# Ordering a tile's twelve matmuls by precision part, and moving four low-rank terms from VectorE to ScalarE and an accumulating store

## The reference

```python
def reference(x, itok_B_3_7, itok_B_0_15, L0_cond_A, L0_cond_B, L1_cond_W, L1_cond_lora_A, L1_cond_lora_B):
    ...
    x = x + _L0_cond_ref(x, L0_cond_A, L0_cond_B, itok_B_3_7)
    x = x + _L1_cond_ref(x, itok_B_0_15, L1_cond_W, L1_cond_lora_A, L1_cond_lora_B)
    return x
```

## Time and profile before

| | us |
|---|---|
| median of 3 runs | 1306.52 |
| lowest, highest | 1306.44, 1308.64 |
| the profiled execution | 1306.84 |
| its span, first to last instruction | 1305.1 |
| TensorE busy | 1293.8 (99%) |
| VectorE busy | 957.0 (73%) |
| ScalarE busy | 459.3 (35%) |
| GpSimd busy | 161.5 (12%) |

### The profile page before, as it was taken

How to read it: one execution, slowest core, us unless ns; L and a number is a source line. 1 busy time by engine, 2 the same in 40 slices (tenths; PEclk the granted TensorE clock), 3 DMA queues, 4 the chain that set the end, 5 groups by cost and what they waited for, 6 DMA issues and landing times.

```text
span 1305.1 us, 15493 instructions
## 1 busy us (share of the span) xinstructions
PE 1293.8 (99%) x5716; PEld 1068.6 (82%) x5716; DVE 957.0 (73%) x1031; ACT 459.3 (35%) x540; POOL 161.5 (12%) x277
## 2 busy tenths in 40 slices
PE   9999999999999999999999999999999999999998
PEld 7888888888888888888888888887888888888776
DVE  4547766556684786877677866769898887778998
ACT  3322222222234422332232443334433344444451
POOL 3001120111033210001201100111000110100021
PEclk9999999999999999999999999999999999999999
DMA  8786877669999965668978473572965987868577
GB/s 282 273 295 198 312 255 223 230 220 320 358 350 236 288 225 194 210 225 298 360 239 314 160 258 121 190 253 99 262 220 197 369 261 212 229 168 264 122 202 201
DMA packets 87549, 316.33 MB, mean 242 GB/s; under 512 B 15650, under 2 KB 15650, under 8 KB 81074
## 3 DMA queue, kind: packets, MB, share of 16 engines
q1 hardware_dynamic: 61010, 246.44, 54.7%
q0 software_dynamic: 26464, 68.90, 19.1%
HBM read 213.48 MB, written 102.83 MB: 242 GB/s over the span
## 4 chain that ended last, share of the span: by engine, by line
PE 85%; DVE 8%; DMA 2%; issue 2%; ACT 1%; POOLq 0%; POOL 0%; DVEq 0%; ACTq 0%
PE ps L1340 42%; PE ps L2510 33%; PE ps L1289 3%; PE ps L1247 2%; PE ps L2466 2%; DVE xq L2241 1%; PE ps L1268 1%; DVE b_lo L2260 1%; DMA out_y<-stage 1%; DVE w_lo L2254 1%; PE ps L2452 1%; DMA out_y<-stage_all 1%; DVE uq L2285 1%; DVE xq L2228 1%; DVE stage L2288 0%
## 5 line engine op out<-in xcount | busy, mean ns | idle before, releaser
L1340 PE MATMUL ps<-b_hi,w_hi 128*128 128x512 f32 x888 | 345.8, 389 | 0.4 <-DVE w_lo L968 0.4
L1340 PE MATMUL ps<-b_hi,w_lo 128*128 128x512 f32 x888 | 345.5, 389 | 0.0
L1340 PE MATMUL ps<-b_lo,w_hi 128*128 128x512 f32 x888 | 345.4, 389 | 0.0
L2510 PE MATMUL ps<-b_hi,w_hi 128*128 128x512 f32 x784 | 305.7, 390 | 3.0 <-DVE w_lo L2254 1.5
L2510 PE MATMUL ps<-b_hi,w_lo 128*128 128x512 f32 x784 | 305.1, 389 | 0.0
L2510 PE MATMUL ps<-b_lo,w_hi 128*128 128x512 f32 x784 | 305.0, 389 | 0.0
L1340 PEld LDWEIGHTS ps<-b_hi,w_hi 128*128 128x128 f32 x888 | 166.7, 188 | 35.7 <-DVE w_lo L968 1.3
L1340 PEld LDWEIGHTS ps<-b_hi,w_lo 128*128 128x128 f32 x888 | 166.7, 188 | 34.9
L1340 PEld LDWEIGHTS ps<-b_lo,w_hi 128*128 128x128 f32 x888 | 166.7, 188 | 34.6
L2087 ACT CAST w_hi<-wq 128x1024 fp32r<-128x1024 f32 x98 | 103.4, 1055 | 210.3 <-PE ps L2510 197.4
L2510 PEld LDWEIGHTS ps<-b_hi,w_hi 128*128 128x128 f32 x784 | 147.1, 188 | 35.6 <-DVE w_lo L2254 2.3
(11 more groups left out here) (186 smaller groups left out, 1283.6 us busy)
## 6 DMA issues: line engine op xcount, KB each, us to landing
x_raw<-in_xT SPq DMA_DIRECT2D x56, 512.0 KB, 6.9
wq<-w_ops SPq DMA_DIRECT2D x28, 1024.0 KB, 5.0
w_raw<-in_W SPq DMA_DIRECT2D x55, 512.0 KB, 6.0
xq<-in_xT SPq DMA_DIRECT2D x44, 512.0 KB, 6.1
out_y<-stage POOLq DMA_DIRECT2D x38, 512.0 KB, 5.7
w_sum<-x_raw SPq DMA_DIRECT2D x24, 512.0 KB, 8.4
out_y<-stage_all POOLq DMA_DIRECT2D x48, 256.0 KB, 6.2
wq<-w_sum SPq DMA_DIRECT2D x12, 1024.0 KB, 7.4
```

Of the source, the lines that this page charges most:

```text
L1340: last = pe.matmul(bank[:, :], w[n % 2][:, c, t * P:(t + 1) * P], x[:, 2 * j + c, :], start=(j == 0 and c == 0 and w is w_hi and x is b_hi ...
L2510: last = pe.matmul(out, w[:, h, c, col:col + P], b[x], start=(po in (Q1, Q2, Q5, Q3) and c == 0 and i == 0), stop=(c == 3 and i == 2), ski ...
```

## The change

Two parts, both in `two_level`.

1. In the first tile of each unit (t even) TensorE runs its 12 matmuls as four of high x high, four of low weights x high input, four of high weights x low input. It waits for w_hi and b_hi of the whole unit at the start, for w_lo before the fifth and for b_lo before the ninth matmul. In the second tile the order stays as it was.
2. The four low-rank terms of batch 6, tiles 0 to 3 (they belong to C11 of the last outer product; units (M5, 3) and (M5, 4)) change from kind "u2" to kind "hbm". VectorE's four `lr_add` go, ScalarE copies the four tiles, and GpSimd adds them to y by two accumulating stores, which stand three units after the matmul, in (M5, 6) and (M5, 7), and wait until both of C11's stores of y have landed (`u_stored[c]` at 32). `fin` of C11 no longer waits for `lr_add`.

```diff
+    fix_plan += [(6, 2 * h, unit(M5, 3 + h)) for h in range(2)]
...
-    for c, place in ((C11, 6), (C22, 10), (C12, 18), (C21, 22)):
+    for c, place in ((C22, 10), (C12, 18), (C21, 22)):
...
             pool.wait_ge(lr_copied, 2 * f + 2)
-            pool.wait_ge(stage_stored[GROUP[M2][c]][h], 16 * stage_stores(M2, c, h))
+            if b > 5:
+                pool.wait_ge(u_stored[c], 32)
+            else:
+                pool.wait_ge(stage_stored[GROUP[M2][c]][h], 16 * stage_stores(M2, c, h))
...
-                    if use[2] == n - 1:
+                    if use[2] == n - (3 if use[0] > 5 else 1):
                         store_fix(f)
...
-            dve.wait_ge(*sides(M5, c, h, False))
+            if c != C11:
+                dve.wait_ge(*sides(M5, c, h, False))
...
-                pe.wait_ge(w_ready, F + n + 1)
...
-                    for c in range(4):
-                        if t == 0 and c % 2 == 0:
-                            pe.wait_ge(x_ready, X0 + 2 * q + c // 2 + 1)
-                        if c == 3:
+                    hi, x_lo, w_lo_ = (w_hi, b_hi), (w_hi, b_lo), (w_lo, b_hi)
+                    if t % 2:
+                        terms = [(c, *pair) for c in range(4) for pair in (hi, x_lo, w_lo_)]
+                    else:
+                        terms = [(c, *pair) for pair in (hi, w_lo_, x_lo) for c in range(4)]
+                        pe.wait_ge(w_hi_done, F + n + 1)
+                        pe.wait_ge(x_hi_done, X0 + 2 * q + 2)
+                    for i, (c, w, b) in enumerate(terms):
+                        if t % 2 == 0 and i == 4:
+                            pe.wait_ge(w_ready, F + n + 1)
+                        if t % 2 == 0 and i == 8:
+                            pe.wait_ge(x_ready, X0 + 2 * q + 2)
+                        if i == 9:
                             for s in lr_here(n, t % 2, "bank"):
                                 lr_mm(s, out)
```

More of the change, by code:

```diff
@@ L2500, in rest @@
                             pe.wait_ge(*pair)
-                    for c in range(4):
-                        if t == 0 and c % 2 == 0:
-                            pe.wait_ge(x_ready, X0 + 2 * q + c // 2 + 1)
-                        if c == 3:
+                    hi, x_lo, w_lo_ = (w_hi, b_hi), (w_hi, b_lo), (w_lo, b_hi)
[11 more added lines that the diff above has]
+                        if i == 9:
                             for s in lr_here(n, t % 2, "bank"):
                                 lr_mm(s, out)
-                        x = (slice(None), 2 * (q % 2) + c // 2, c % 2, slice(None))
                         col = t % 2 * P
[L2509 to L2512, removed]
+                        last = pe.matmul(out, w[:, h, c, col:col + P], b[:, 2 * (q % 2) + c // 2, c % 2, :],
+                                         start=(po in (Q1, Q2, Q5, Q3) and i == 0), stop=(i == 11),
+                                         skip_group_check=po in CHAIN or mo in (M4, M5))
                     last.then_inc(tile_done, 1)
```

## The result

The changed kernel takes **1313.22 us** (median of 8 runs, 1311.02 to 1315.26) against 1306.48 for the kernel before in the same comparison (8 runs, 1306.32 to 1309.11). The ratio is 1.0045, with a 95% interval of 1.0037 to 1.0054: slower by 5.9 us (the two medians alone differ by 6.7). The profiled execution took 1313.49 us, 1311.5 of them in the span.

What follows compares the result with a forecast made beforehand. TensorE, busy 1293.8 of 1305.1 us, bounds the kernel, with VectorE's queue setting the end from 1260 us. A late load's +4.2 less 0.97 gained gives +3.2 over 1306.52: 1309.7 us, range 1304.0 to 1312.8.

Steps and rivals of the forecast that it cites:

- High parts first: First tiles: w_lo gaps at (M7, 1) and (M5, 5) close, -0.97 and -1.02 us; waits already met cost 0.
- from this part alone: At (M5, 5): the new matmul order by itself closes the w_lo gap, -1.02 us.
- C11 to ScalarE, relief of VectorE: In M5: 2.4 us leave VectorE's queue, its lead shrinks to 1.1 us, and an earlier store of stage gives 0.3.
- The landing of C11's second store of y: On GpSimd's queue: it lands at 1261.9 instead of 1264.2, bounds 1260.0 and 1263.0.
- GpSimd's issue: The first accumulating store is issued at 1262.0, right behind the landing at 1261.9.
- From the store's issue to load 13's landing: Load 13 (low-rank weights, batch 7, third quarter) lands 9.2 us after the accumulating store's issue, at 1271.2.
- Here only wq: Beside the late load SP runs only wq, not xq and wq as at 924, so 9.2 us, under 11.15.
- Everything behind VectorE's split is late by the same: VectorE splits at 1271.9 instead of 1267.70, +4.2 us on the queue that sets the end; ScalarE and TensorE wait within it.
- The sum: Whole kernel: 4.2 us delay less 0.97 gained in M7, 3.2 us slower; M5's gains of 1.1 and 0.3 are swallowed.
- full contention: Rival, chance 0.11: load 13 lands at 1274.2, delay 7.2 less 0.97, +6.2 us, 1312.7 us.
- delay and gain cancel at a landing of 1268.0: Load 13's landing where the sign changes; the cancelling rival, chance 0.26, had it land at 1268.2: +0.2, 1306.7 us.

Runs made afterwards that it cites:

- e1: Kernel before with only the matmul order changed, C11's terms left on VectorE: 1306.18 us against 1306.50.
- e10: Changed kernel without the two accumulating stores and their waits (y lacks those terms): 1304.81 us against 1306.70 for the kernel before.
- e8: e1 with C11's first store of y moved behind its second store of stage and a low-rank load on GpSimd: 1305.14 us against 1306.66 before.
- e4: Changed kernel without the two accumulating stores but with their waits kept (y lacks those terms): 1309.30 us against 1306.50 for the kernel before.
- e2: Kernel before with only C11's low-rank terms moved, matmul order as before: 1316.11 us against 1306.50.
- e5: Changed kernel with GpSimd issuing the loads ahead of the two accumulating stores within a unit: 1311.60 us against 1306.66 for the kernel before.
- e3: Changed kernel with the two accumulating stores moved to (M5, 11) and (M5, 12): 1308.05 us against 1306.50 for the kernel before.
- e6: Changed kernel with both accumulating stores in (M5, 8), right behind load 14: 1306.97 us against 1306.66 for the kernel before.
- e7: e6 with C11's first store of y moved behind its second store of stage and a low-rank load on GpSimd: 1306.29 us against 1306.66 before.
- e11: The changed kernel measured once more, unaltered, on the chip of e10: 1313.09 us against 1306.70 for the kernel before.

## Why the prediction was right and where it was too small

The direction and the mechanism were as predicted: the load behind the wait is late, and that is the loss. The size was too small. The median is 3.5 us above the forecast and 0.4 above the range's upper end; by the ratio, 1306.5 x 1.0045 = 1312.4, the change is just inside it. Step by step:

- **High parts first.** Right. The gaps at (M7, 1) and (M5, 5) are gone, no other first tile of e1 shows a break, so waits that are met cost nothing here, and -1.00 in the trace of e1 stands against -0.97. The -1.02 of (M5, 5) "from this part alone" closes the gap but never reaches the end: that sentence was local, and e1 shows it.
- **C11 to ScalarE, relief of VectorE.** The mechanism (lead lost behind ScalarE) was right, the size not: 1.1 + 0.3 was predicted, 0.5 is left (e10 against e1, in the trace). VectorE's work went earlier, but it waits for the landing of a store, and that store, issued 3.25 us earlier in e10, took 1.4 us longer (11.8 against 10.4). Why is open: in e8, issued 8.9 us earlier, it took 9.7.
- **The landing of C11's second store of y.** Predicted 1261.9 in the time of the profile before. The changed profile runs 0.57 earlier here (0.97 gained, 0.40 lost ahead of 903), so 1261.3; measured 1261.5.
- **GpSimd's issue.** Taken as 0.1 us behind the landing; it was 0.54 (1261.51 to 1262.05).
- **From the store's issue to load 13's landing.** This is the term that was mis-sized most: 9.2 taken, between 7.1 and 11.15, and 10.58 measured (1262.05 to 1272.63). "Here only wq" was argued to make it cheap; but wq, released at 1264.97, took 10.1 us itself, and the window around 1271 shows the DMA engines at a share of 1.02. And wq was not alone. The prediction put one accumulating store ahead of load 13 and nothing of GpSimd's behind it, but the second store, 512 KB, and load 14, 2 x 256 KB, were released by the same landing and left within 2.2 us of load 13. Of these the two stores are worth 2.1 us of its 9.9: without them, with load 14 still there, it takes 7.8 (e4). That the row at 924 us (11.15) comes near 10.58 is partly luck, since other transfers stood beside it. The 0.2, 0.4 and 1.4 of these three steps make the 2.0 us by which VectorE's split is later than forecast.
- **Everything behind VectorE's split is late by the same.** Right for VectorE (5.66 at the split and at the bank), wrong for the end: no step of the prediction had TensorE's clock in it. That is the 0.85 above.
- **The sum.** 2.0 for the transfers, 0.85 for the clock and 0.40 of ordinary difference ahead of 903 in that execution make 3.3, which is 6.5 - 3.2.

Of the rivals, full contention came nearest: its load 13 lands at 1274.2, against 1272.6 + 0.57 = 1273.2 measured in the same frame. That its price, 6.2, meets the trace's +6.13 is luck: the landing was 1.0 too late and the 0.85 was missing. The rule that delay and gain cancel at a landing of 1268.0 can be tried on e4. Load 13 landed at 1268.8 there; in the frame of the prediction (0.97 for the gain in M7, 0.28 for the difference ahead of 903) that is 1270.1, and the rule gives +2.1. The trace says +2.0: the rule holds.

The load of 256 KB took 9.9 us beside the accumulating stores and 7.8 us without them (e4); the first 512 KB store itself took 5.4, the second 12.9. The Trainium skill (DMA: Bandwidth & Descriptors, Anatomy of one DMA) would give 2.6 and 3.2 us, and the trace does not agree in this stretch: of GpSimd's transfers issued from 1245 to 1265 us, in any of the kernels, no load took under 5.7, and stores of 512 KB took 3.8 to 16.2. Later it does: the kernel before's stores of uq at 1275.22 and 1283.63, 512 KB each, took 3.0 and 2.9.

## What to carry to other kernels

A wait put into a queue that also issues loads is priced by the loads behind it: find the landing that the wait adds, add the *loaded* duration of the next transfer, and compare with when that data is needed. Take a transfer's duration from the most crowded comparable row, not from a middle, and list what the same landing releases beside it: here a second store and a load. And before moving work off the engine that sets the end, look at what that engine next waits for: here a store's landing left 0.5 of the 2.4 us taken off VectorE, and issuing that store earlier (e8) was worth as much without moving any work: 0.6 over e1 in the trace.

## What the runs showed of the hardware

- **TensorE's clock after a pause.** After gaps of 7.0 us (changed kernel), 10.0 (e2), 3.85 (e4) and 3.1 (e5) the granted clock was 0.50, 1.2 GHz, for the next matmuls (twelve in the changed kernel, eight in e4); after gaps up to 1.8 us (e3, e6, e7) matmuls kept their 0.227 us. In e4 the fall came only behind the pause: windows of 2 us, while TensorE was already working again:

```profile
1270.00:1272.00 2.00, 0.00 (x0) 0.00 (x0) 1.97 (x3) 1.41 (x2) 0.20 (x1) 1.00 0.74 299
1272.00:1274.00 2.00, 1.76 (x6) 1.45 (x7) 2.00 (x3) 0.00 (x0) 0.77 (x1) 0.79 0.69 63
1274.00:1276.00 2.00, 2.00 (x6) 1.52 (x6) 2.00 (x4) 0.00 (x0) 0.00 (x0) 0.50 0.77 147
```

- **A store's duration depends on its neighbours more than on its bytes.** The same 512 KB of stage took 9.7 us in e8, 10.3 in e1, 11.8 in e10 and 13.0 in e6; and in the kernel before a 512 KB store of uq took 12.1 us issued at 1252.11, in a full stretch, and 3.0 issued at 1275.22.
- **Two executions of one kernel differ by 0.9 us before anything of interest happens** (the same matmul starts at 903.27 in the changed kernel and at 902.40 in e11), so a step of under 1 us is read from the trace behind that point, not from the total.
